# Moving one chunk's statistics of x1 from VectorE to ScalarE in the first stage of a mixing and scan kernel

## The chip, the cores and the metric

One core of a Trainium2 chip. The metric is the device time of one execution in microseconds; lower is better. The kernel before takes 773.96 us (median of 3 runs, 772.08 to 774.88).

## The reference

The input `x` has shape (16, 64, 128, 64): 16 samples, 64 rows h, 128 tokens n, 64 channels. Two layers follow each other, each with a group norm in front and a residual around it:

```
def _gn(v, G=32, eps=1e-05):
    g = v.reshape(B_, H_, W_, G, C_ // G)
    m = jnp.mean(g, axis=(1, 2, 4), keepdims=True)
    s = jnp.var(g, axis=(1, 2, 4), keepdims=True)
    return ((g - m) / jnp.sqrt(s + eps)).reshape(v.shape)

x = x + _L0_conv_ref(_gn(x), centers, spreads, bias)   # posmap (n x n, per head) mixes the tokens
x = x + _L1_conv_ref(_gn(x), conv_W)                   # scan over h: new = row + relu(conv1d(carry, W)), 9 taps
```

The second norm needs mean and variance of x1, the output of the first layer, per sample and pair of channels. These statistics of x1 are what the change is about.

## The kernel before, in words

The batch is worked on in two waves of W = 8 samples. The **first stage** mixes samples 0 to 7 alone, one after the other; the scan over 64 rows of wave 0 then runs while samples 8 to 15 are mixed in its gaps; last comes the scan of wave 1. Every engine has a program written out by hand, and its order is the order of the code; engines meet at semaphores. The change touches the first stage only.

A sample b is cut into CH = 4 chunks of 16 rows h. For each chunk, in this order:

- GpSimd scales the chunk of x by minus the reciprocal deviation of the first norm, in two halves (`scale_half`, L361, tile xs). The first half of a sample waits for `minus_rstd` (L681).
- TensorE mixes the tokens, 4 heads x 2 row halves in two passes (`mix_half`, L916), into `ps_mix` for chunks 0 and 2, into `ps_conv` for chunks 1 and 3.
- VectorE adds bias and residual (`mix_to_x1`, L699), which gives x1 in place.
- TensorE turns the chunk, 8 transposes (`turn_in`, L929, tile `ps_in`). It waits at L926 until ScalarE has emptied `ps_in` of the chunk before.
- ScalarE copies the turned chunk to `x1_paired` and adds the shift of the first norm, 4 activations on 64 partitions x 512 (`keep_in`, L469).
- VectorE takes the statistics of the kept chunk, 2 batch statistics on 128 x 512 (`stats2`, L706, tile st). After 8 of them `moments2` (L712) merges them into mean and variance.

Chunk 3 of a sample is turned and kept during the next sample's chunk 0; its statistics are taken at chunk 1 of the next sample.

Beside that run the statistics of x for a later sample: 16 batch statistics on 128 x 256 (`stats1`, L605), spread over the chunks of VectorE's program. Then comes a short chain for the first norm of sample b + 1: TensorE averages the means (`mean1_of`, after mixing chunk 1), VectorE takes deviations (L664), ScalarE squares them (L432), TensorE averages (`var1_of`, after mixing chunk 2), ScalarE takes the root (L438), VectorE its reciprocal (`guess1_of`, L670), ScalarE squares that (`square1_of`, L443), VectorE gives the ratio (L674) and `minus_rstd` (L681).

What is queued in which order is what matters here:

- ScalarE (L539): keep chunk 3 of b - 1; L432; keep chunk 0; L453; L438; L443; keep chunk 1; L448; keep chunk 2.
- TensorE (`alone_chunk`, L1009): chunk 0: mix 0, turn 3 of the sample before. Chunk 1: mix 1, mean1, turn 0. Chunk 2: mix 2, var1, turn 1, the group mean of b - 1. Chunk 3: mix 3, turn 2, `var2_of`, `shift1_of`. Then mix 0 of the next sample.
- VectorE (`alone_chunk`, L806): x1 of the chunk (L699), then a share of stats1, stats2 and the small steps.

Of the kernel before, what the change touches and what calls it, by code (L numbers as in the profile page):

```python
# [15 lines left out]
def mix_and_scan_kernel(nc: bass.Bass, x: bass.AP, centers: bass.AP, spreads: bass.AP,  # L16
# [5 lines left out]
    ACT = mybir.ActivationFunctionType  # L22
    AX = mybir.AxisListType

    B, H, N, C = x.shape
# [4 lines left out]
    P = 128  # L30
    J = N // 2
# [5 lines left out]
    W = B // 2  # L37
# [5 lines left out]
    CH = 4  # L43
    CR = H // CH
    CC = CR * C
    HR = CR // 2
    RG = 4
    GROUPS = STEPS // RG
    TU = 2 * CH
# [10 lines left out]
    with ExitStack() as ctx:  # L60
        def sb(name, shape, dt=f32):
            return ctx.enter_context(nc.sbuf_tensor(name, shape, dt))
# [4 lines left out]
        def sem(name):  # L67
            return ctx.enter_context(nc.semaphore(name))
# [14 lines left out]
        staged = sb("staged", [P, 2, NS * SW])  # L83
# [9 lines left out]
        minus_mean_rstd = sb("minus_mean_rstd", [P, 2, G, CG])  # L93
        shift1 = sb("shift1", [P, 2])
        st2 = sb("st2", [P, 2 * CH, 6])
        mv = sb("mv", [P, 2])
        dev_c = sb("dev_c", [P, 1])
        dev_c2 = sb("dev_c2", [P, 1])
# [83 lines left out]
        in_turned = sem("in_turned")  # L182
        in_kept = sem("in_kept")
        stats2_done = sem("stats2_done")
        mv_ready = sem("mv_ready")
        mean2_ps = sem("mean2_ps")
        dev_c_ready = sem("dev_c_ready")
# [16 lines left out]
        def x1_unit(wave, b, c, u):  # L204

            if wave == 1:
                v = x1_paired[:, bass.ds(b * (H * J) + (c * CR + u * HR) * J, HR * J)]
                return v.rearrange("p (h j) -> p h j", j=J)
            v = x1_paired[:, :].rearrange("p (h w j) -> p h w j", w=W, j=J)
            v = v[:, c * CR + u * HR:c * CR + (u + 1) * HR, bass.ds(b, 1), :]  # L210
            return v.rearrange("p h w j -> p h (w j)")

        def x1_chunk(wave, b, c):

            if wave == 1:
                v = x1_paired[:, bass.ds(b * (H * J) + c * CR * J, CR * J)]
                return v.rearrange("p (h j) -> p h j", j=J)
            v = x1_paired[:, :].rearrange("p (h w j) -> p h w j", w=W, j=J)
            return v[:, c * CR:(c + 1) * CR, b, :]
# [9 lines left out]
        def buf_of(b):  # L229

            return XB - 1 - b % XB
# [9 lines left out]
        def alone(eng, done):  # L241

            eng.wait_ge(done, 1)

        def held(eng, n):

            return n if isinstance(n, int) else eng.to_reg(n)

        def is_zero(n):
            return isinstance(n, int) and n == 0  # L250
# [173 lines left out]
        def _(act):  # L424
            for s in range(S):
                act.wait_ge(score_ready, s + 1)
                nc.scalar.activation(prob[:, s, :], score[:, s, :], ACT.Exp, bias=neg_max[:, s:s + 1],
                                     accum_out=exp_sum[:, s:s + 1]).then_inc(prob_ready, 1)
# [12 lines left out]
            def square1_of(b, halves=1):  # L441
                act.wait_ge(guess1_ready, b + 1)
                nc.scalar.activation(square1[:, :], guess1[:, :], ACT.Square,  # L443
                                     scale=math.sqrt(0.5 * halves / COUNT)).then_inc(square1_ready, 1)
# [8 lines left out]
                nc.scalar.activation(shift2[:, bass.ds(b, 1)], minus_mean2[:, :], ACT.Copy,  # L453
                                     scale=rstd2[:, bass.ds(b, 1)]).then_inc(shift2_ready, 1)

            def keep_in(b, k, wave, bw, c, first, count, free):

                if first == 0:
                    act.wait_ge(shift1_ready, b + 1)
                    chunks = held(act, b * CH + c + 1)  # L460
                    alone(act, setup_done)
                    if free is not None:
                        for s in range(NS):
                            act.wait_ge(total_ready[s], free)
                    act.wait_ge(in_turned, chunks)
                dst = x1_chunk(wave, bw, c)
                for r, q in ((0, 0), (0, 1), (1, 0), (1, 1))[first:first + count]:
                    src = ps_in[r * C:(r + 1) * C, :].rearrange("p (k j q) -> p q k j", k=HR, q=2)
                    ins = nc.scalar.activation(dst[q * C:(q + 1) * C, r:CR:2, :], src[:, q, :, :],  # L469
                                               ACT.Identity, bias=shift1[r * C:(r + 1) * C, k:k + 1])  # L470
                if first + count == 4:
                    ins.then_inc(in_kept, 1)

            def prep(b, e, i, prev, it):

# [63 lines left out]
            for b in range(W):  # L539
                if b > 0:  # L540
                    keep_in(b - 1, (b - 1) % 2, 0, b - 1, CH - 1, 0, 4, None)
                dev2_of(b + 1)
                keep_in(b, b % 2, 0, b, 0, 0, 4, None)
                if b > 1:
                    shift2_of(b - 2)
                std1_of(b + 1)
                square1_of(b + 1)
                keep_in(b, b % 2, 0, b, 1, 0, 4, None)
                if b > 0:
                    dev_c2_of(b - 1)  # L550
                keep_in(b, b % 2, 0, b, 2, 0, 4, None)
# [34 lines left out]
        def _(dve):  # L586
            nc.vector.memset(w_raw, 0.0).then_inc(w_zeroed, 1)
            nc.vector.memset(eps_col[:, :], EPS)
            nc.vector.memset(half_power[:, :], -0.5).then_inc(consts, 1)
            nc.vector.memset(ones_row, 1.0)  # L590
            nc.vector.memset(inv_p[:, :], 1.0 / P)
# [7 lines left out]
            def stats1(b, e, first, count):  # L599

                for c in range(CH):
                    dve.wait_ge(x_loaded[e][c], 16 * (b // XB + 1) if isinstance(b, int) and b <= W else 8 * b - 16 + 8 * e)
                v = x_bufs[e].rearrange("p (h m g e) -> p m h e g", m=G // 2, g=2, e=CG)
                for m in range(first, first + count):
                    ins = nc.vector.bn_stats(st1[:, 0, 2 * m:2 * m + 2, :].rearrange("p g k -> p (g k)"),  # L605
                                             v[:, m, :, :, :])
                if first + count == G // 2:
                    ins.then_inc(stats1_done, 1)
# [59 lines left out]
            def guess1_of(b):  # L668
                dve.wait_ge(std1_ready, b + 1)
                nc.vector.reciprocal(guess1[:, :], std1[:, :]).then_inc(guess1_ready, 1)  # L670
# [24 lines left out]
            def mix_to_x1(b, e, c, ps):  # L695
# [3 lines left out]
                nc.vector.scalar_tensor_tensor(v, ps[:, :].rearrange("p (s n) -> p n s", s=S),  # L699
                                               bias_col[:, 0:1], v, ALU.add, ALU.add).then_inc(x1_done, 1)  # L700

            def stats2(b, wave, bw, c, u):
                if c == 0 and u == 0 and not is_zero(b):
                    dve.wait_ge(mv_ready, b)
                dve.wait_ge(in_kept, b * CH + c + 1)
                nc.vector.bn_stats(st2[:, 2 * c + u, :], x1_unit(wave, bw, c, u)).then_inc(stats2_done, 1)  # L706

            def moments2(b):
                seen = held(dve, TU * b + TU)
                alone(dve, consts)  # L710
                dve.wait_ge(stats2_done, seen)
                nc.vector.bn_aggr(mv[:, :], st2[:, :, :].rearrange("p n k -> p (n k)")).then_inc(mv_ready, 1)  # L712

            def deviations2(b, wave):
                dve.wait_ge(mean2_ps, b + 1)
# [90 lines left out]
            def alone_chunk(b, c):  # L806

                e = buf_of(b)
                mix_to_x1(b, e, c, (ps_mix, ps_conv)[c % 2])
                nb, ne, nk = b + 1, buf_of(b + 1), (b + 1) % 2  # L810
                ahead = b + 2 <= W
                ae = buf_of(b + 2)
                if c == 0:
                    if b == 0:
                        stats1(nb, ne, 0, 9)
                    stats1(nb, ne, 9, 4)
                    if b > 0:
                        stats2(b - 1, 0, b - 1, 2, 0)
                        stats2(b - 1, 0, b - 1, 2, 1)
                    stats1(nb, ne, 13, 3)  # L820
                if c == 1:
                    dev_of(nb)
                    if b > 0:
                        stats2(b - 1, 0, b - 1, 3, 0)
                        stats2(b - 1, 0, b - 1, 3, 1)
                        moments2(b - 1)
                if c == 2:
                    stats2(b, 0, b, 0, 0)
                    guess1_of(nb)
                    if b > 0:  # L830
                        deviations2(b - 1, 0)
                    stats2(b, 0, b, 0, 1)
                    ratio1_of(nb)
                    if ahead:
                        stats1(b + 2, ae, 0, 1)
                    rstd1_of(nb, nk)
                    if ahead:
                        stats1(b + 2, ae, 1, 3)
                if c == 3:
                    mean_rstd1(nb, nk)  # L840
                    if ahead:
                        stats1(b + 2, ae, 4, 3)
                    stats2(b, 0, b, 1, 0)
                    if b > 0:
                        variance2(b - 1, 0)
                    stats2(b, 0, b, 1, 1)
                    keep_shift1(nb, nk)
                    if ahead:
                        stats1(b + 2, ae, 7, 2)

            dev_of(0, 2)
            guess1_of(0)
# [224 lines left out]
```

## Time and profile before

| | |
|---|---|
| median of 3 runs | 773.96 us |
| the profiled execution | 779.17 us, its span 777.4 us |
| busy over the span: TensorE, VectorE, ScalarE, GpSimd | 88%, 76%, 63%, 55% |
| first mixed chunk of sample 0 reaches VectorE | 29.5 us |
| first step of the scan on VectorE (L789) | 185.55 us |

The span is that of the profiled core, from the first instruction to the last; the execution's own time is 1.8 us longer, and it lies 5.2 us above the median. A group of instructions is given with its line, engine, operation, `output<-input`, shape and count. "Idle before" is the time its engine waited just ahead of it, with the instruction that released it. The granted clock is a share of full speed: 1.00 is 2.4 GHz, 0.50 is 1.2 GHz.

### The profile page before, as it was taken

To read this page: it belongs to the slowest core of one execution; us is meant where nothing else is said; L and a number is where in the kernel's file an instruction comes from. 1 tells how busy PE (TensorE), PEld (TensorE's weight loads), DVE (VectorE), ACT (ScalarE), POOL (GpSimd) and SP (SyncE) were. 2 spreads that over 40 slices of the span, in tenths; PEclk is the share of its full clock that TensorE was granted. 3 is DMA by queue.
4 is the path that set the end of the run, shared out by engine and by line. 5 is a ranking of instruction groups with operands and counts; after the bars stand their busy time and mean duration, and the time that the engine had idled before them with its cause. 6 is when DMAs were issued, how large, how long until landed. Compare 5 with 4: busy or idle time off the path is not lost.

```text
span 777.4 us, 18263 instructions
## 1 busy us (share of the span) xinstructions
PE 682.4 (88%) x5100; PEld 645.6 (83%) x5100; DVE 592.8 (76%) x1426; ACT 490.2 (63%) x854; POOL 431.0 (55%) x416
## 2 busy tenths in 40 slices
PE   1577777767999999999899999996999999999996
PEld 1466666657899898989799898995999999999995
DVE  7578999983878888797879888765666776776774
ACT  1165777776676777676676777746666666666661
POOL 1555556642666666665566666661555555555554
PEclk9888999997999999999999999998999999999999
DMA  9844656231455554554555543331444444444444
GB/s 185 155 109 109 134 113 134 55 82 30 80 104 102 107 105 77 106 98 85 98 100 101 106 79 50 52 53 28 70 75 73 72 69 76 72 68 75 72 72 78
DMA packets 412050, 68.18 MB, mean 88 GB/s; under 512 B 411988, under 2 KB 411988, under 8 KB 411988
## 3 DMA queue, kind: packets, MB, share of 16 engines
q1 hardware_dynamic: 359764, 61.17, 42.5%
q10 hardware_dynamic: 52224, 6.30, 5.2%
q8 instruction: 24, 0.39, 0.2%
q14 instruction: 38, 0.31, 0.2%
HBM read 33.85 MB, written 33.55 MB: 87 GB/s over the span
## 4 chain that ended last, share of the span: by engine, by line
PE 46%; DVE 23%; issue 13%; ACTq 6%; ACT 6%; SPq 3%; POOL 1%; DVEq 1%; DMA 0%; POOLq 0%
PE ps_conv L992 22%; PE ps_conv L996 11%; DVE st L605 7%; PE ps_mix L916 7%; ACTq L503 6%; PE ps_in L929 5%; DVE carry L789 3%; DVE st L706 3%; SPq L299 3%; DVE carry_l L799 2%; ACT carry_h L513 2%; DVE staged L776 2%; PE ps_small L906 2%; ACT x_paired L469 2%; DVE x_sb L699 2%
## 5 line engine op out<-in xcount | busy, mean ns | idle before, releaser
L388 POOL TENSOR_TENSOR total<-x_paired,carry 128x256 f32<-128x256 f32 x256 | 252.2, 985 | 237.8 <-DVE staged L776 230.6
L513 ACT ACTIVATE carry_h<-carry 128x256 fp32r<-128x256 f32 x252 | 105.3, 418 | 188.1 <-DVE carry L789 136.7
L491 ACT ACTIVATE rows<-x_paired,shift,rstd 128x256 f32 (+1 forms) x256 | 213.6, 843 | 0.2
L992 PE MATMUL ps_conv<-carry_h,wh 128*128 128x256 f32 x1280 | 204.7, 291 | 6.7 <-ACT carry_h L513 6.3
L996 PE MATMUL ps_conv<-carry_l,wh 128*128 128x256 f32 x1280 | 194.2, 282 | 0.3 <-DVE carry_l L799 0.3
L469 ACT ACTIVATE x_paired<-ps_in,shift 64x512 f32<-64x512 f32 (+1 forms) x256 | 174.8, 683 | 31.2 <-PE ps_in L929 26.6
L992 PE MATMUL ps_conv<-carry_h,wl 128*128 128x256 f32 x1280 | 194.2, 282 | 0.0
L992 PEld LDWEIGHTS ps_conv<-carry_h,wh 128*128 128x128 f32 x1280 | 171.4, 191 | 11.4 <-ACT carry_h L513 9.4
L799 DVE TENSOR_TENSOR carry_l<-carry,carry_h 128x256 fp32r<-128x256 f32 x252 | 134.6, 534 | 58.9 <-ACT carry_h L513 41.9
L992 PEld LDWEIGHTS ps_conv<-carry_h,wl 128*128 128x128 f32 x1280 | 171.4, 190 | 0.0
L996 PEld LDWEIGHTS ps_conv<-carry_l,wh 128*128 128x128 f32 x1280 | 170.7, 189 | 0.6 <-DVE carry_l L799 0.6
L361 POOL TENSOR_TENSOR xs<-x_sb,minus_rstd 128x512 f32<-128x512 f32 x104 | 139.8, 1356 | 45.7 <-DVE minus_rstd L681 34.1
L789 DVE SCALAR_TENSOR_TENSOR carry<-ps_conv,rows 128x256 f32<-128x256 f32 x256 | 106.7, 417 | 74.2 <-PE ps_conv L996 62.8
L776 DVE STREAM_TRANSPOSE staged<-total 128x256 f32<-128x256 f32 x256 | 110.7, 433 | 5.4 <-DMA out_dram<-staged 5.0
L916 PE MATMUL ps_mix<-xs,mix 128*128 128x256 f32 x384 | 105.3, 407 | 0.6 <-DVE x_sb L699 0.4
L706 DVE BATCH_NORM_STATS2 st<-x_paired 128x6 f32<-128x512 f32 (+1 forms) x128 | 85.7, 683 | 8.2 <-ACT x_paired L469 8.2
L916 PEld LDWEIGHTS ps_mix<-xs,mix 128*128 128x128 f32 x384 | 71.6, 202 | 9.7 <-POOL xs L361 1.8
L605 DVE BATCH_NORM_STATS2 st<-x_sb 128x6 f32<-128x256 f32 x208 | 73.8, 405 | 0.0
L929 PE MATMUL ps_in<-ident,x_sb 128*128 128x128 f32 x416 | 55.9, 278 | 15.7 <-ACT x_paired L469 11.4
L929 PEld LDWEIGHTS ps_in<-ident,x_sb 128*128 128x128 f32 x416 | 48.6, 145 | 22.2 <-issue 17.9
L699 DVE SCALAR_TENSOR_TENSOR x_sb<-ps_mix,bias_col,x_sb 128x1024 f32<-128x1024 f32 x42 | 53.6, 1276 | 5.9 <-PE ps_mix L916 5.8
L361 POOL TENSOR_TENSOR xs<-rows,minus_rstd 128x512 f32<-128x512 f32 x24 | 31.2, 1335 | 33.1 <-DVE minus_rstd L681 31.7
(89 smaller groups left out, 290.2 us busy)
## 6 DMA issues: line engine op xcount, KB each, us to landing
x_sb<-in_x_dram SPq DMA_DIRECT2D x52, 512.0 KB, 4.1
out_dram<-staged SPq DMA_DIRECT2D x832, 32.0 KB, 1.6
rows<-in_x_dram SPq DMA_DIRECT2D x12, 512.0 KB, 4.0
out_dram<-staged ACTq DMA_DIRECT2D x192, 32.0 KB, 1.8
x_paired<-in_L_conv_W_dram SPq DMA_DIRECT2D x2, 80.0 KB, 2.9
x_paired<-in_L_conv_W_dram SPq DMA_DIRECT2D x2, 64.0 KB, 2.6
x_paired<-v_attention_centers_dram SPq DMA_DIRECT2D x1, 0.0 KB
x_paired<-v_attention_spreads_dram SPq DMA_DIRECT2D x1, 0.0 KB
```

The source lines that it names most:

```text
L361: nc.gpsimd.tensor_tensor(xs[:, c % 2, heads, :, :].rearrange("p s h v -> p h v s"), src, minus_rstd1[:, k, m:G:2].unsqueeze(1).unsqueeze( ...
L388: nc.gpsimd.tensor_tensor(total[s][:, :].rearrange("p (w j) -> p w j", w=WS), x1_rows(wave, it, i, 1, s * WS, WS)[:, 0, :, :], carry[s][:, ...
L469: ins = nc.scalar.activation(dst[q * C:(q + 1) * C, r:CR:2, :], src[:, q, :, :], ACT.Identity, bias=shift1[r * C:(r + 1) * C, k:k + 1])
L491: nc.scalar.activation(rows[:, g % 2, :, w // WS, :, w % WS], x1_rows(wave, it, g * RG, RG, w, 1)[:, :, 0, :], ACT.Identity, scale=rstd2[: ...
L605: ins = nc.vector.bn_stats(st1[:, 0, 2 * m:2 * m + 2, :].rearrange("p g k -> p (g k)"), v[:, m, :, :, :])
L776: nc.vector.transpose(staged[:, buf, s * SW:(s + 1) * SW], total[s][:, :]).then_inc(out_flipped[s], 1)
L789: nc.vector.scalar_tensor_tensor(carry[s][:, :], ps_conv[:, s * BANK:s * BANK + SW], 0.0, rows[:, (i // RG) % 2, i % RG, s, :, :].rearrang ...
L799: nc.vector.tensor_tensor(carry_l[s][:, EDGE:EDGE + J, :].rearrange("p j w -> p (j w)"), carry[s][:, :], carry_h[s][:, EDGE:EDGE + J, :].r ...
L916: ins = nc.tensor.matmul(ps[:, s * CR * V:(s + 1) * CR * V], mix[:, s, :], xs[:, c % 2, s, :, :].rearrange("p h v -> p (h v)"), start=True ...
L929: ins = nc.tensor.transpose(ps_in[:, k * P:(k + 1) * P], x_bufs[e][:, at:at + P], ident[:, :])
L992: nc.tensor.matmul(ps_conv[:, s * BANK:s * BANK + SW], w[:, d, :], carry_h[s][:, d:d + J, :].rearrange("p j w -> p (j w)"), start=(w is wh ...
L996: ins = nc.tensor.matmul(ps_conv[:, s * BANK:s * BANK + SW], wh[:, d, :], carry_l[s][:, d:d + J, :].rearrange("p j w -> p (j w)"), start=F ...
```

## The change

In the first stage the statistics of chunk 0 of each sample move to ScalarE. The 4 activations that keep chunk 0 also give their sums (`accum_out`, each to a column of `sums2`). A new step, `squares2`, stands in ScalarE's program behind `square1_of` and ahead of the copy of chunk 1: it scales the two sums to means, written into the statistics tile st2 (slot 0 or 7 by turns); it waits for that; then two activations on 128 x 512 square the kept chunk about its mean and give the sums of squares, also into st2. The squared values go to `staged`, which is not used in this stage. VectorE no longer takes chunk 0's two batch statistics, and merges 7 slots in place of 8: six of its own and one from ScalarE. VectorE's stats1 are placed anew: three more of them stand in chunk 2, and one fewer before the copy of the shift in chunk 3. The second wave is as it was.

```diff
-            def keep_in(b, k, wave, bw, c, first, count, free):
+            def keep_in(b, k, wave, bw, c, first, count, free, sums=None):
...
                     ins = nc.scalar.activation(dst[q * C:(q + 1) * C, r:CR:2, :], src[:, q, :, :],
-                                               ACT.Identity, bias=shift1[r * C:(r + 1) * C, k:k + 1])
+                                               ACT.Identity, bias=shift1[r * C:(r + 1) * C, k:k + 1],
+                                               accum_out=None if sums is None else sums[q * C:(q + 1) * C, r:r + 1])
                 if first + count == 4:
                     ins.then_inc(in_kept, 1)
+
+            def squares2(b):
+
+                slot = (TU - 1) * (b % 2)
+                act.wait_ge(in_kept, b * CH + 1)
+                if b > 1:
+                    act.wait_ge(mv_ready, b - 1)
+                nc.scalar.activation(st2[:, slot, 1:6:3], sums2[:, :], ACT.Copy,
+                                     scale=1.0 / (HR * J)).then_inc(mean_c_ready, 1)
+                act.wait_ge(mean_c_ready, b + 1)
+                for r in range(2):
+                    nc.scalar.activation(staged[:, r, :], x1_chunk(0, b, 0)[:, r:CR:2, :],
+                                         ACT.Square, scale=-1.0, bias=st2[:, slot, 1 + 3 * r:2 + 3 * r],
+                                         accum_out=st2[:, slot, 2 + 3 * r:3 + 3 * r]).then_inc(squares2_done, 1)
...
-                keep_in(b, b % 2, 0, b, 0, 0, 4, None)
+                if b > 0:
+                    act.wait_ge(squares2_done, 2 * b)
+                keep_in(b, b % 2, 0, b, 0, 0, 4, None, sums2)
                 if b > 1:
                     shift2_of(b - 2)
                 std1_of(b + 1)
                 square1_of(b + 1)
+                squares2(b)
                 keep_in(b, b % 2, 0, b, 1, 0, 4, None)
...
             def moments2(b):
-                seen = held(dve, TU * b + TU)
+                first, last = 0, TU
+                seen = held(dve, TU * b + TU - 2 * W)
+                if wave_chunk(b):
+                    seen = (TU - 2) * (b + 1)
+                    first, last = b % 2, TU - 1 + b % 2
                 alone(dve, consts)
+                if wave_chunk(b):
+                    dve.wait_ge(squares2_done, 2 * (b + 1))
                 dve.wait_ge(stats2_done, seen)
-                nc.vector.bn_aggr(mv[:, :], st2[:, :, :].rearrange("p n k -> p (n k)")).then_inc(mv_ready, 1)
+                nc.vector.bn_aggr(mv[:, :], st2[:, first:last, :].rearrange("p n k -> p (n k)")).then_inc(mv_ready, 1)
...
                 if c == 2:
-                    stats2(b, 0, b, 0, 0)
                     guess1_of(nb)
+                    if ahead:
+                        stats1(b + 2, ae, 0, 3)
                     if b > 0:
                         deviations2(b - 1, 0)
-                    stats2(b, 0, b, 0, 1)
+                    if ahead:
+                        stats1(b + 2, ae, 3, 1)
                     ratio1_of(nb)
                     if ahead:
-                        stats1(b + 2, ae, 0, 1)
+                        stats1(b + 2, ae, 4, 1)
                     rstd1_of(nb, nk)
                     if ahead:
-                        stats1(b + 2, ae, 1, 3)
+                        stats1(b + 2, ae, 5, 1)
```

VectorE's order at chunk 2 of a sample, from x1 of chunk 2 to x1 of chunk 3, before:

```order
L699 SCALAR_TENSOR_TENSOR x_sb<-ps_mix,bias_col,x_sb 128x1024
L706 BN_STATS st<-x_paired 128x6
L670 RECIPROCAL guess<-std 128x32
L718 TENSOR_TENSOR dev_c<-mv,ps_out 128x1
L719 TENSOR_SCALAR minus_mean<-ps_out 128x1
L706 BN_STATS st<-x_paired 128x6
L674 SCALAR_TENSOR_TENSOR ps_small<-ps_small,square 128x32
L605 BN_STATS st<-rows 128x6
L681 SCALAR_TENSOR_TENSOR minus_rstd<-ps_small,guess 128x32
L605 BN_STATS st<-rows 128x6 x3
L699 SCALAR_TENSOR_TENSOR x_sb<-ps_conv,bias_col,x_sb 128x1024
```

The same place in the changed kernel (its line numbers are larger, L721 for L699, L692 for L670):

```order
L721 SCALAR_TENSOR_TENSOR x_sb<-ps_mix,bias_col,x_sb 128x1024
L692 RECIPROCAL guess<-std 128x32
L627 BN_STATS st<-rows 128x6 x3
L750 TENSOR_TENSOR dev_c<-mv,ps_out 128x1
L751 TENSOR_SCALAR minus_mean<-ps_out 128x1
L627 BN_STATS st<-rows 128x6
L696 SCALAR_TENSOR_TENSOR ps_small<-ps_small,square 128x32
L627 BN_STATS st<-rows 128x6
L703 SCALAR_TENSOR_TENSOR minus_rstd<-ps_small,guess 128x32
L627 BN_STATS st<-rows 128x6
L721 SCALAR_TENSOR_TENSOR x_sb<-ps_conv,bias_col,x_sb 128x1024
```

The two statistics of x1 are gone, one of them from in front of the reciprocal; six statistics of x stand here in place of four, four of them between the reciprocal and the ratio.

ScalarE's order from the copy of chunk 0 to the copies of chunks 2 and 3, before:

```order
L469 ACTIVATE x_paired<-ps_in,shift 64x8x64 x4
L453 ACTIVATE shift<-minus_mean,rstd 128x1
L438 ACTIVATE std<-ps_small,eps_col 128x32
L443 ACTIVATE square<-guess 128x32
L469 ACTIVATE x_paired<-ps_in,shift 64x8x64 x4
L448 ACTIVATE dev_c<-dev_c 128x1
L469 ACTIVATE x_paired<-ps_in,shift 64x8x64 x8
```

And in the changed kernel:

```order
L472 ACTIVATE x_paired,sums<-ps_in,shift 64x8x64 x4
L456 ACTIVATE shift<-minus_mean,rstd 128x1
L441 ACTIVATE std<-ps_small,eps_col 128x32
L446 ACTIVATE square<-guess 128x32
L484 ACTIVATE st<-sums 128x2
L488 ACTIVATE staged,st<-x_paired,st 128x512 x2
L472 ACTIVATE x_paired<-ps_in,shift 64x8x64 x4
L451 ACTIVATE dev_c<-dev_c 128x1
L472 ACTIVATE x_paired<-ps_in,shift 64x8x64 x8
```

Three activations, and a wait for the first of them, now stand between the square of the guess and the copy of chunk 1.

## Rows read from the trace of the kernel before

**Rows 1.** One sample of the first stage: busy us per engine (count); clock share, DMA.
```profile
104.94:121.97 17.03, 12.65 (x78) 10.78 (x78) 16.36 (x39) 12.16 (x22) 10.69 (x10) 1.00 0.57 124
```

**Rows 2.** The chain of waits in the same stretch, shares by line.
```profile
by line: DVE st L605 28.6%; issue 20.1%; DVE x_sb L699 15.2%; DVE st L706 12.5%; PE ps_in L929 9.3%; PE ps_mix L916 8.3%; PE ps_small L906 1.8%; DVEq L602 1.3%; DVE minus_mean_rstd L686 0.9%; DVE ps_small L674 0.9%; DVE minus_rstd L681 0.8%
```

**Rows 3.** Timeline, samples 4 to 5: start us, duration us, engine, line, operation, [idle before <-releaser].
```profile
111.26 2.77 ACT L469 ACTIVATE x_paired<-ps_in,shift 64x512 f32<-64x512 f32 x4
...
112.89 1.28 DVE L699 SCALAR_TENSOR_TENSOR x_sb<-ps_mix,bias_col,x_sb 128x1024 f32<-128x1024 f32 x1 [0.25 <-PE ps_mix L916]
...
114.13 0.69 DVE L706 BATCH_NORM_STATS2 st<-x_paired 128x6 f32<-128x512 f32 x1
...
114.74 0.34 DVE L670 RECIPROCAL guess<-std 128x32 f32<-128x32 f32 x1
...
115.11 0.23 ACT L443 ACTIVATE square<-guess 128x32 f32<-128x32 f32 x1 [0.45 <-DVE guess L670]
...
115.36 2.77 ACT L469 ACTIVATE x_paired<-ps_in,shift 64x512 f32<-64x512 f32 x4
...
116.81 5.08 POOL L361 TENSOR_TENSOR xs<-x_sb,minus_rstd 128x512 f32<-128x512 f32 x4 [6.04 <-DVE minus_rstd L681]
...
118.27 1.06 PE L929 MATMUL ps_in<-ident,x_sb 128*128 128x128 f32 x8 [1.08 <-ACT x_paired L469]
...
119.45 2.77 ACT L469 ACTIVATE x_paired<-ps_in,shift 64x512 f32<-64x512 f32 x4 [1.10 <-PE ps_in L929]
...
119.76 1.97 PE L916 MATMUL ps_mix<-xs,mix 128*128 128x256 f32 x8
...
121.97 1.27 DVE L699 SCALAR_TENSOR_TENSOR x_sb<-ps_mix,bias_col,x_sb 128x1024 f32<-128x1024 f32 x1
...
123.55 2.76 ACT L469 ACTIVATE x_paired<-ps_in,shift 64x512 f32<-64x512 f32 x4 [1.33 <-PE ps_in L929]
...
126.87 0.38 PE L906 MATMUL ps_small<-st,inv_p 128*128 128x32 f32 x2 [1.71 <-DVE st L605]
...
128.30 2.77 ACT L469 ACTIVATE x_paired<-ps_in,shift 64x512 f32<-64x512 f32 x4
```

**Rows 4.** Groups by line over the whole span: count | busy, mean ns | idle before.
```profile
L513 ACT ACTIVATE carry_h<-carry 128x256 fp32r<-128x256 f32 x252 | 105.3, 418 | 188.1 <-DVE carry L789 136.7
L491 ACT ACTIVATE rows<-x_paired,shift,rstd 128x256 f32 (+1 forms) x256 | 213.6, 843 | 0.2
...
L706 DVE BATCH_NORM_STATS2 st<-x_paired 128x6 f32<-128x512 f32 (+1 forms) x128 | 85.7, 683 | 8.2 <-ACT x_paired L469 8.2
```

**Rows 5.** Timeline of ScalarE in the setup, activations that also sum.
```profile
8.39 0.39 ACT L427 ACTIVATE x_paired<-x_paired 128x128 f32<-128x128 f32 x1
8.68 0.19 ACT L427 ACTIVATION_READ_ACCUMULATOR x_paired<-x_paired 128x1 f32 x1
8.78 0.39 ACT L427 ACTIVATE x_paired<-x_paired 128x128 f32<-128x128 f32 x1
```

**Rows 6.** Timeline of samples 0 and 1, around chunk 1's copy.
```profile
43.08 0.34 DVE L670 RECIPROCAL guess<-std 128x32 f32<-128x32 f32 x1
...
43.45 0.23 ACT L443 ACTIVATE square<-guess 128x32 f32<-128x32 f32 x1 [1.52 <-DVE guess L670]
...
46.48 1.25 PE L929 MATMUL ps_in<-ident,rows 128*128 128x128 f32 x8 [2.13 <-ACT x_paired L469]
...
51.22 1.28 DVE L699 SCALAR_TENSOR_TENSOR x_sb<-ps_mix,bias_col,x_sb 128x1024 f32<-128x1024 f32 x1 [1.48 <-PE ps_mix L916]
```

**Rows 7.** Timeline one sample on.
```profile
65.88 1.06 PE L929 MATMUL ps_in<-ident,x_sb 128*128 128x128 f32 x8 [1.84 <-ACT x_paired L469]
...
70.86 1.28 DVE L699 SCALAR_TENSOR_TENSOR x_sb<-ps_mix,bias_col,x_sb 128x1024 f32<-128x1024 f32 x1 [1.53 <-PE ps_mix L916]
```

**Rows 8.** TensorE's busy time and granted clock in one stretch of 2 us.
```profile
68.00:70.00 2.00, 2.00 (x6) 0.50 1.07 243
```

**Rows 9.** Timeline of TensorE behind the last sample of the stage.
```profile
173.50 1.93 PE L929 MATMUL ps_in<-ident,x_sb 128*128 128x128 f32 x8 [2.47 <-ACT x_paired L469]
```

More of the change, by code:

```diff
@@ L95, in mix_and_scan_kernel @@
         st2 = sb("st2", [P, 2 * CH, 6])
+        sums2 = sb("sums2", [P, 2])
         mv = sb("mv", [P, 2])
@@ L184, in mix_and_scan_kernel @@
         stats2_done = sem("stats2_done")
+        mean_c_ready = sem("mean_c_ready")
+        squares2_done = sem("squares2_done")
         mv_ready = sem("mv_ready")
@@ L588, in _ @@
             nc.vector.memset(eps_col[:, :], EPS)
+            nc.vector.memset(st2[:, 0:TU:TU - 1, 0:6:3], HR * J)
             nc.vector.memset(half_power[:, :], -0.5).then_inc(consts, 1)
@@ L700, in mix_to_x1, with wave_chunk @@
                                                bias_col[:, 0:1], v, ALU.add, ALU.add).then_inc(x1_done, 1)
+            def wave_chunk(b):
+                return 1 if isinstance(b, int) and b < W else 0
             def stats2(b, wave, bw, c, u):
-                if c == 0 and u == 0 and not is_zero(b):
+                if c == wave_chunk(b) and u == 0 and not is_zero(b):
                     dve.wait_ge(mv_ready, b)
                 dve.wait_ge(in_kept, b * CH + c + 1)
-                nc.vector.bn_stats(st2[:, 2 * c + u, :], x1_unit(wave, bw, c, u)).then_inc(stats2_done, 1)
+                nc.vector.bn_stats(st2[:, 2 * c + u - wave_chunk(b), :], x1_unit(wave, bw, c, u)).then_inc(stats2_done, 1)
             def moments2(b):
-                seen = held(dve, TU * b + TU)
+                first, last = 0, TU
[3 more added lines that the diff above has]
+                    first, last = b % 2, TU - 1 + b % 2
                 alone(dve, consts)
+                if wave_chunk(b):
+                    dve.wait_ge(squares2_done, 2 * (b + 1))
                 dve.wait_ge(stats2_done, seen)
-                nc.vector.bn_aggr(mv[:, :], st2[:, :, :].rearrange("p n k -> p (n k)")).then_inc(mv_ready, 1)
+                nc.vector.bn_aggr(mv[:, :], st2[:, first:last, :].rearrange("p n k -> p (n k)")).then_inc(mv_ready, 1)
             def deviations2(b, wave):
@@ L841, in alone_chunk @@
                     if ahead:
-                        stats1(b + 2, ae, 4, 3)
+                        stats1(b + 2, ae, 6, 3)
                     stats2(b, 0, b, 1, 0)
@@ L847, in alone_chunk @@
                     keep_shift1(nb, nk)
-                    if ahead:
-                        stats1(b + 2, ae, 7, 2)
             dev_of(0, 2)
```

## The prediction

> **What bounds the kernel now.** I read three views, all in the first stage, because the change touches nothing behind it. The table of stretches says how full each engine is over one sample: the sample takes 17.03 us, VectorE is busy 16.36 of them (96%), ScalarE 12.16, TensorE 12.65, GpSimd 10.69, the clock is full [rows 1]. The chain of waits gives the same picture: VectorE's statistics and x1 steps hold most of it, and ScalarE does not appear [rows 2]. So far VectorE looks like the bound, and taking two statistics from it like a gain.
>
> The third view is the timeline of one sample [rows 3], read for what waits behind ScalarE. Its four copies stand 4.1 us apart (111.26, 115.36, 119.45, 123.55) and the last gap is 4.75 us (to 128.30). In every 4.1 us, 2.77 are the copy itself and the rest is the turning of the next chunk, which may not begin before the copy ends: 115.36 + 2.77 = 118.13, and TensorE starts turning at 118.27 after 1.08 us idle, released by ScalarE. This ring of ScalarE and TensorE needs 4 x 4.1 = 16.4 us per sample, 96% of the period too. And TensorE's queue holds more behind that turning: the small products, then the mix of the next sample's chunk 0 at 119.76, ready at 121.73. VectorE takes it at 121.97, so the mix was 0.24 us early, and with a pick-up of some 0.05 us the slack is **0.2 us**. From there VectorE needs until about 126.7 for the last statistic of x, TensorE follows at 126.87 (released by it), turns chunk 0, and ScalarE starts on it at 128.30. That closes a second ring: copy 0, square of the guess, copy 1, turning of chunk 2, mix of chunk 0, x1, statistics of x, turning of chunk 0. It passes through both engines, and only 0.2 us of it is slack.
>
> **What the change removes.** Two batch statistics at L706 per sample, 683 ns each in the row [rows 4], about 0.60 us each from start to start (the reciprocal follows the statistic of 114.13 at 114.74 [rows 3]): 1.2 us per sample. Where they stood, between x1 of chunk 2 and the ratio, VectorE lies in the second ring only by the reciprocal. The reciprocal of 114.74 waits for ScalarE's root, which starts behind the copy and ends about 114.67, so taking the statistic from in front of it returns 0.1 us at most; I take nothing. In samples 0 and 1 the reciprocal was late through VectorE itself: ScalarE's square had been idle 1.52 us ahead of it [rows 6]. There the removed statistic gives back 0.6 us, once in each.
>
> **What it adds, all on ScalarE.**
> - Sums of the four copies. In the setup an activation that sums is followed by a read of the accumulator: 8.39, 8.68, then 8.78 [rows 5]. The read adds 0.10 us from start to start; its own duration is 0.19, which is the upper end. 4 x 0.10 = 0.40.
> - The scaling to means and the wait for it. The nearest small activation takes 0.23 us (at 115.11 [rows 3]). I take 0.23.
> - Two squares of 128 x 512. L513 takes 418 ns for 256 columns, L491 843 ns for 256 columns written with a stride [rows 4], and the copy L469 2.77 / 4 = 0.69 for 512. Source and target of the squares lie in runs of 64 and more, as the copy's do, so I take 0.61 from start to start plus 0.10 for the read: 1.42 for both. Upper end, at L491's rate: 2 x (1.69 + 0.19) = 3.8.
>
> The sum is 0.40 + 0.23 + 1.42 = **2.05 us** per sample, all of it ahead of copy 1, so on both rings. Per sample:
> - Samples 2 to 6: 2.05 less the slack of 0.2 is 1.85, times five 9.25.
> - Samples 0 and 1: the sums (0.40) lie in ScalarE's wait for the guess, and 0.6 comes back: 2.05 - 0.40 - 0.60 = 1.05 each, 2.1.
> - Sample 7: behind it ScalarE keeps copying and normalising up to the scan's first step, so 2.05 in full.
>
> That makes 13.4 us. Moved work costs nothing: the six statistics of x that now stand at chunk 2 delay `minus_rstd` and with it GpSimd's first half by some 0.9 us against copy 0. GpSimd's halves start at 116.81 and take 5.08 / 4 = 1.27 each, so chunk 0 is scaled at 119.4 while TensorE reaches it at 119.76; TensorE now comes 2.05 later and GpSimd about 1.3 (0.4 of the sums and 0.9), so it stays early. If not, this would cost up to its 0.9 us per sample. The one memset added in the setup and the merge over 7 slots I take as nothing. There is no new DMA.
>
> **TensorE's clock.** TensorE's idle time ahead of the turning of chunk 2 was 1.08 us [rows 3]. It grows by 2.05 less the 0.40 by which mixing chunk 3 also moves: **2.7 us**. What such a pause did in this trace: after 2.13 us [rows 6] and 1.84 us [rows 7] at this very place, and after 2.47 us behind the last sample [rows 9] (1.93 us there for 8 transposes that take 1.06), TensorE ran at the lower level, 0.50 or 1.2 GHz [rows 8]; after 1.71 us (ahead of 126.87 [rows 3]) it did not. The price stands in the time from turning to x1: 51.22 - 46.48 = 4.74 and 70.86 - 65.88 = 4.98 against 121.97 - 118.27 - 0.2 = 3.5, so 1.24 and 1.48 us, mean 1.36. In samples 0 and 1 it is paid already; six pauses are new. I expect the lower level in part of them, as the fall does not always meet the mix of chunk 0, and take 3.3 of six: 4.5 us. None would be 0, all six 8.2.
>
> **Sum.** 13.4 + 4.5 = 17.9 us. The profiled execution would go from 779.17 to 797.1, and the median, 5.2 us below it, from 773.96 to **791.9**.
>
> **Rivals.**
> - *The clock holds.* The period of one sample grows to 18.9 us but the mix stays at 2.4 GHz: 774.0 + 13.4 = 787.4. For it: the full-clock periods with a pause of 1.71 us each. Against: three of the four long pauses above. With an insertion at 1.9 us it would be 786.
> - *VectorE is the bound, and its relief counts.* 8 x 1.2 = 9.6 us less: 764.4. For it: 96% busy and the chain of waits [rows 1, 2]. The Trainium skill (Perfetto Trace Analysis, Identifying the Most-Contended Engine, and Optimizing Scalar/DVE Operations) says the engine with the highest occupancy is the one to work on first, and that handing work to ScalarE may pay once VectorE is saturated; this case's busy shares fit that rule. Against: ScalarE's insertion would have to cost less than the 0.2 us of slack, or stand off both rings; it stands ahead of copy 1, and copy 1 releases TensorE. The point from which this decides is ScalarE's time between the square and copy 1: under 0.2 us VectorE's gain shows, above it ScalarE's loss.
> - *Loss and gain cancel*, because part of ScalarE's 4.87 us idle per sample (17.03 - 12.16) takes up the insertion: about 772. Against: that idle time is waiting for the turning, which itself waits for the copy.
> - *The squares are slow*, at L491's rate: 3.8 in place of 1.42, so 8 x 2.4 = 19 us more: 807 to 811. Against: the copy at L469 writes the same tile at 0.69.
> - *The change doesn't do what it says*: excluded, the order shows two statistics per sample gone and three activations added.
>
> **Chances.** Path longer and clock lower in part: 0.62. Clock holds: 0.22. Slow squares: 0.07. Cancel: 0.05. Relief counts: 0.04. A measurement of this kernel can tell about 0.5% (3.9 us) from no change. Faster by over that: 0.04; within: 0.05; slower: 0.91. The range takes in the two likeliest cases with their bounds: low 13.4 with an insertion of 1.9 (less 1.2) and no lower clock, 786, less 2 for the spread of the runs; high 13.4 + 8.2 and reads at 0.14 in place of 0.10 (6 x 0.04 x 8 = 2), 798, plus 2. So 784 to 800.
>
> **What would show it.** The distance of x1 of chunk 0 from sample to sample: 18.9 at full clock, 20.3 with the lower one, in place of 17.03. VectorE's busy share of a sample under 85%, with idle time ahead of the reciprocal (about 1 us) and ahead of x1 of chunk 0 (over 1 us), which had none. TensorE idle 2.7 us ahead of turning chunk 2. The group of squares at 0.70 us each. The scan's first step near 203 in place of 185.55, and nothing changed behind it. Wrong I would be if copy 1 began as early as before, that is if the squares had found idle time, or if the period stayed at 17 us.

## The result, and the profile after

The changed kernel takes 801.97 us (median of 4 runs, 799.3 to 802.71) against 774.42 us of the kernel before on the same chip: 1.0351 times as long, 95% interval 1.0312 to 1.0389, so 27.55 us slower. The sign was as forecast. The forecast was 791.9 us with a range of 784 to 800, so the loss was 1.5 times the 17.9 us forecast and the time lies above the range.

The profiled execution took 802.71 us, its span 800.9 us. The scan's first step on VectorE begins at 211.87 us; it was at 185.55. So the first stage lost 26.3 us, and behind it the two profiles differ by 2.8 us the other way (591.8 and 589.0 us). The loss by samples, from x1 of chunk 0 to that of the next sample:

| sample | before, us | after, us | difference |
|---|---|---|---|
| 0 | 21.72 | 22.93 | 1.21 |
| 1 | 19.64 | 22.56 | 2.92 |
| 2 | 17.05 | 20.64 | 3.59 |
| 3, 4 | 17.03 | 20.63 | 3.60 each |
| 5 | 17.04 | 21.42 | 4.38 |
| 6 | 17.03 | 21.94 | 4.91 |
| 7 and on to the scan | 29.51 | 31.62 | 2.11 |

The table of stretches of the changed kernel, for samples 3, 5 and 6 (us, then busy time and count of TensorE, its weight loads, VectorE, ScalarE, GpSimd; granted clock; share and GB/s of DMA), answers to [rows 1]:

```profile
95.63:116.26 20.63, 14.14 (x80) 12.09 (x79) 15.38 (x36) 14.26 (x30) 10.71 (x9) 0.92 0.48 103
...
136.89:158.31 21.42, 16.32 (x80) 13.79 (x79) 15.25 (x37) 14.26 (x30) 10.71 (x9) 0.81 0.47 99
158.31:180.25 21.94, 16.51 (x80) 14.28 (x79) 15.39 (x36) 14.26 (x30) 10.75 (x9) 0.81 0.11 24
```

VectorE's busy time fell from 16.36 to 15.38 us, ScalarE's rose from 12.16 to 14.26, as intended. But the sample takes 20.63 us, and neither engine is near that. The granted clock, 1.00 before, is 0.92 and 0.81.

The chain of waits over sample 3 answers to [rows 2]. ScalarE did not appear in it; its copies now hold the largest share:

```profile
by line: ACT x_paired L472 24.7%; PE ps_mix L948 18.9%; issue 17.9%; DVE st L627 11.5%; PE ps_in L961 9.6%; ACT staged L488 4.5%; DVE st L732 3.5%; PE ps_small L938 3.2%; DVE guess L692 1.8%; PE ps_out L938 1.6%; ACT shift L456 1.4%; ACT st
```

The timeline of that sample answers to [rows 3 to 5] (start us, duration us, engine, line, operation, idle time before and its releaser):

```profile
101.97 0.68 ACT L472 ACTIVATE x_paired<-ps_in,shift 64x512 f32<-64x512 f32 x1
102.55 0.19 ACT L472 ACTIVATION_READ_ACCUMULATOR x_paired<-ps_in,shift 64x1 f32 x1
102.76 0.68 ACT L472 ACTIVATE x_paired<-ps_in,shift 64x512 f32<-64x512 f32 x1
...
103.45 0.20 ACT L472 ACTIVATION_READ_ACCUMULATOR x_paired<-ps_in,shift 64x1 f32 x1
...
103.66 0.69 ACT L472 ACTIVATE x_paired<-ps_in,shift 64x512 f32<-64x512 f32 x1
...
105.37 0.30 ACT L456 ACTIVATE shift<-minus_mean,rstd 128x1 f32<-128x1 f32 x1
...
106.01 0.35 DVE L692 RECIPROCAL guess<-std 128x32 f32<-128x32 f32 x1 [1.14 <-ACT std L441]
...
106.40 0.23 ACT L446 ACTIVATE square<-guess 128x32 f32<-128x32 f32 x1 [0.42 <-DVE guess L692]
...
106.54 0.19 ACT L484 ACTIVATE st<-sums 128x2 f32<-128x2 f32 x1
...
106.76 0.72 ACT L488 ACTIVATE staged<-x_paired,st 128x512 f32<-128x512 f32 x1
...
107.48 0.71 ACT L488 ACTIVATE staged<-x_paired,st 128x512 f32<-128x512 f32 x1
...
108.18 2.75 ACT L472 ACTIVATE x_paired<-ps_in,shift 64x512 f32<-64x512 f32 x4
...
108.35 5.08 POOL L364 TENSOR_TENSOR xs<-x_sb,minus_rstd 128x512 f32<-128x512 f32 x4 [7.52 <-DVE minus_rstd L703]
...
111.08 1.06 PE L961 MATMUL ps_in<-ident,rows 128*128 128x128 f32 x8 [2.57 <-ACT x_paired L472]
...
112.26 2.77 ACT L472 ACTIVATE x_paired<-ps_in,shift 64x512 f32<-64x512 f32 x4 [1.10 <-PE ps_in L961]
...
112.62 3.61 PE L948 MATMUL ps_mix<-xs,mix 128*128 128x256 f32 x8
...
116.26 1.28 DVE L721 SCALAR_TENSOR_TENSOR x_sb<-ps_mix,bias_col,x_sb 128x1024 f32<-128x1024 f32 x1 [2.92 <-PE ps_mix L948]
```

Read it down ScalarE. From the first activation of copy 0 to L456 it was 2.80 us before; now it is 105.37 - 101.97 = 3.40. From the square of the guess to copy 1 it was 0.25; now it is 108.18 - 106.40 = 1.78. These two, 0.60 and 1.53, are the insertion: **2.13 us**. VectorE waits 1.14 us for the root, and later for the mix. TensorE is idle 2.57 us ahead of turning chunk 2 (111.08), still turns at full speed, and then mixes chunk 0 in 3.61 us where it took 1.97. From turning to x1 that makes 116.26 - 111.08 = 5.18 us, where it was 3.70.

Two groups of the profile's page: copies as before at 683 ns, and 16 batch statistics fewer, at the duration they had [rows 4].

```profile
L472 ACT ACTIVATE x_paired<-ps_in,shift 64x512 f32<-64x512 f32 (+1 forms) x256 | 174.9, 683 | 41.0 <-PE ps_in L961 36.8
...
L732 DVE BATCH_NORM_STATS2 st<-x_paired 128x6 f32<-128x512 f32 (+1 forms) x112 | 75.0, 684 | 9.5 <-ACT x_paired L472 9.2
```

### The profile page after: what moved, and what is told of

Its sections match the earlier page's. It is cut to its first block, busy times and chain, and to the rows that moved or that the text cites. A ratio compares the mean times of both kernels' runs of the same rounds, so it can differ in the third digit from the quotient of the medians.

```text
span 800.9 us, 18347 instructions
## 1 busy us (share of the span) xinstructions
PE 696.3 (87%) x5100; PEld 659.0 (82%) x5100; DVE 585.6 (73%) x1411; ACT 507.0 (63%) x926; POOL 431.3 (54%) x416
## 4 chain that ended last, share of the span: by engine, by line
PE 46%; DVE 18%; issue 14%; ACT 11%; ACTq 6%; SPq 3%; POOL 1%; DVEq 1%; DMA 0%; POOLq 0%
PE ps_conv L1024 21%; PE ps_conv L1028 10%; PE ps_mix L948 8%; ACTq L521 6%; DVE st L627 6%; ACT x_paired L472 5%; PE ps_in L961 5%; DVE carry L821 3%; SPq L302 3%; ACT carry_h L531 2%; PE ps_small L938 2%; DVE carry_l L831 2%; DVE st L732 2%; DVE staged L808 2%; ACT rows L509 2%
## 5 line engine op out<-in xcount | busy, mean ns | idle before, releaser
L948 PE MATMUL ps_mix<-xs,mix 128*128 128x256 f32 x384 | 114.0, 434 | 0.2 <-POOL xs L364 0.2
L948 PEld LDWEIGHTS ps_mix<-xs,mix 128*128 128x128 f32 x384 | 77.8, 219 | 11.4 <-POOL xs L364 1.4
L732 DVE BATCH_NORM_STATS2 st<-x_paired 128x6 f32<-128x512 f32 (+1 forms) x112 | 75.0, 684 | 9.5 <-ACT x_paired L472 9.2
L961 PE MATMUL ps_in<-ident,x_sb 128*128 128x128 f32 x416 | 58.0, 285 | 21.9 <-ACT x_paired L472 20.5
L961 PEld LDWEIGHTS ps_in<-ident,x_sb 128*128 128x128 f32 x416 | 50.6, 149 | 28.0 <-issue 18.4
L721 DVE SCALAR_TENSOR_TENSOR x_sb<-ps_mix,bias_col,x_sb 128x1024 f32<-128x1024 f32 x42 | 53.6, 1277 | 19.1 <-PE ps_mix L948 19.0
```

What stands on the lines that cost most here:

```text
L948: ins = nc.tensor.matmul(ps[:, s * CR * V:(s + 1) * CR * V], mix[:, s, :], xs[:, c % 2, s, :, :].rearrange("p h v -> p (h v)"), start=True ...
L961: ins = nc.tensor.transpose(ps_in[:, k * P:(k + 1) * P], x_bufs[e][:, at:at + P], ident[:, :])
```

## The experiments

Each time is a median of the kernel's runs, and each ratio is to the kernel before, measured beside it: 776.25 us for the first four kernels, 774.93 us for the last four. Times of samples are those of the one profiled execution.

### Filling TensorE's pause

On the changed kernel:

```diff
+                if c == 3:
+                    pe.wait_ge(x1_done, b * CH + 3)
+                    for s in range(S):
+                        nc.tensor.matmul(ps_mix[:, 0:256], mix[:, s, :],
+                                         mix[:, 0:2, :].rearrange("p s m -> p (s m)"), start=True, stop=True)
                 if c > 0:
                     turn_in(b, buf_of(b), c - 1)
```

> The changed kernel with four products of 256 columns (0.49 us each, 1.97 us) that nobody reads, on TensorE ahead of turning chunk 2 in the first stage. They fill the pause of 2.57 us. Theory (the path is longer by 2.11 us, and the pause takes TensorE to 1.2 GHz just where the mix of chunk 0 is on the path): the granted clock stays at 1.00, samples 2 to 6 stand 18.9 us apart in place of 20.6 to 21.9, and the time is 774.4 + 13.8 = 788, or 1 to 3 less if samples 0 and 1 keep the clock too. Rival (the clock is not what costs 12 us; some wait on ScalarE or GpSimd is longer than I read): it stays at 800 to 804, for the fillers only use idle time.

Measured: 788.92 us, 1.0173 times before (1.0133 to 1.0213), as expected. More work on TensorE took 13 us off the changed kernel. Its timeline in sample 3, then the table of stretches for the next sample:

```profile
101.04 1.89 PE L1056 MATMUL ps_mix<-mix 128*128 128x256 f32 x8
...
103.78 1.07 PE L961 MATMUL ps_in<-ident,rows 128*128 128x128 f32 x8 [0.84 <-ACT x_paired L472]
...
105.27 1.97 PE L948 MATMUL ps_mix<-xs,mix 128*128 128x256 f32 x8
...
107.28 1.28 DVE L721 SCALAR_TENSOR_TENSOR x_sb<-ps_mix,bias_col,x_sb 128x1024 f32<-128x1024 f32 x1 [1.24 <-PE ps_mix L948]
```

```profile
107.28:126.22 18.94, 14.38 (x86) 12.31 (x86) 15.38 (x36) 14.24 (x31) 10.72 (x9) 1.00 0.50 112
```

The unread products (101.04) leave 0.84 us of pause, the mix of chunk 0 takes 1.97 us again, and the granted clock is 1.00. Samples 2 to 6 take 18.94 us each. So two losses are told apart: 18.94 - 17.03 = 1.91 us per sample is the longer path at full clock, and the rest of the 3.6 to 4.9 us hung on the clock. Samples 0 and 1 became 1.67 and 3.94 us shorter than in the changed kernel (21.26 and 18.62 us), so there too the clock had cost time.

### The same work on ScalarE, in its waits

On the changed kernel, `squares2` split in two by `r`, with the scaling in the first part:

```diff
                 square1_of(b + 1)
-                squares2(b)
                 keep_in(b, b % 2, 0, b, 1, 0, 4, None)
                 if b > 0:
                     dev_c2_of(b - 1)
+                squares2(b, 0)
                 keep_in(b, b % 2, 0, b, 2, 0, 4, None)
+                squares2(b, 1)
```

> The changed kernel with the same work on ScalarE in another place: the scaling to means and the first square after copy 1 and L451, the second square after copy 2, where ScalarE waits 1.1 to 1.3 us for the next turning. Theory (place on the ring decides): only the four reads of the accumulator, 0.60 us, stay ahead of copy 1. Less the slack of 0.2 that is 0.4 in five samples, nothing or a gain of 0.5 in samples 0 and 1, some 1.3 in sample 7, and TensorE's pause stays near 1.1 us, so the clock holds: 775 to 779. Rival (ScalarE's added load costs wherever it stands): 800 to 802. Rival (VectorE's relief then shows): 766 to 770.

Measured: 777.68 us, 1.0023 times before (1.0004 to 1.0042). The sum of ScalarE's work is the same as in the changed kernel, and 24 us of the loss are gone. The timeline of sample 3 shows why:

```profile
95.03 0.23 ACT L446 ACTIVATE square<-guess 128x32 f32<-128x32 f32 x1 [0.42 <-DVE guess L694]
...
95.30 2.77 ACT L472 ACTIVATE x_paired<-ps_in,shift 64x512 f32<-64x512 f32 x4
...
98.20 0.19 ACT L485 ACTIVATE st<-sums 128x2 f32<-128x2 f32 x1
98.21 1.06 PE L963 MATMUL ps_in<-ident,rows 128*128 128x128 f32 x8 [1.08 <-ACT x_paired L472]
...
98.42 0.72 ACT L489 ACTIVATE staged<-x_paired,st 128x512 f32<-128x512 f32 x1
...
99.39 2.77 ACT L472 ACTIVATE x_paired<-ps_in,shift 64x512 f32<-64x512 f32 x4 [0.16 <-PE ps_in L963]
...
101.71 1.28 DVE L723 SCALAR_TENSOR_TENSOR x_sb<-ps_mix,bias_col,x_sb 128x1024 f32<-128x1024 f32 x1 [0.77 <-PE ps_mix L950]
...
102.19 0.72 ACT L489 ACTIVATE staged<-x_paired,st 128x512 f32<-128x512 f32 x1
```

The square of the guess (95.03) is followed by copy 1 after 0.27 us, and TensorE's pause ahead of turning chunk 2 is 1.08 us, as before the change. Scaling and first square stand at 98.20 and 98.42. The copy of chunk 2 (99.39) still starts 1.18 us behind the turning, having waited 0.16 us for it; in the kernel before it had waited 1.10. Four of samples 2 to 6 take 17.45 us, 0.42 more than before. Against VectorE's relief alone (16.85, the next experiment) they take 0.60 more: the four accumulator reads in full, and nothing for scaling and squares. So work of ScalarE is free where its engine waits for the turning, and costs in full where the turning waits for it.

Two things lie behind the near zero of the total. Samples 0 and 1 were 1.9 and 2.2 us shorter than before (19.82 and 17.46 us), which hides a part of what the reads cost. And one sample, 4, took 18.28 us: TensorE's mix of chunk 1 took 3.55 us in it (at 112.61) in place of 1.97, behind a pause of only 1.57 us.

### VectorE's relief alone

On the changed kernel, without sums, scaling and squares, so that chunk 0 of samples 0 to 7 is left out of the second norm's statistics:

```diff
-                squares2(b)
...
-                    act.wait_ge(squares2_done, 2 * b)
-                keep_in(b, b % 2, 0, b, 0, 0, 4, None, sums2)
+                keep_in(b, b % 2, 0, b, 0, 0, 4, None)
...
-                    first, last = b % 2, TU - 1 + b % 2
+                    first, last = 1, TU - 1
...
-                    dve.wait_ge(squares2_done, 2 * (b + 1))
```

> The changed kernel without anything new on ScalarE: chunk 0 of samples 0 to 7 is left out of the second norm's statistics, and VectorE has the changed order. Theory (two rings, VectorE's relief is worth only the slack of ScalarE's ring): 0.2 us in five samples and 0.6 in samples 0 and 1, 772, at most 770. Rival (VectorE is the bound): 8 x 1.2 = 9.6 less, 765.

Measured: 771.41 us, 0.995 times before (0.993 to 0.997), 4.8 us less. The scan's first step:

```profile
179.85 0.42 DVE L816 SCALAR_TENSOR_TENSOR carry<-ps_conv,rows 128x256 f32<-128x256 f32 x1 [1.93 <-ACT rows L509]
```

It comes 5.70 us earlier than the 185.55 before, so the gain lies in the first stage. The period of a sample:

```profile
99.80:116.65 16.85, 12.65 (x78) 10.78 (x78) 15.16 (x37) 12.17 (x22) 10.71 (x10) 1.00 0.56 125
```

VectorE's busy time is down by 1.20 us per sample, the period by 0.18 (16.85 against 17.03), the slack of 0.2 us. That rules out the rival by which the relief counts in full. Most of the gain stands in samples 0 and 1, which became 1.58 and 2.80 us shorter (20.14 and 16.84 us) where 0.6 us each was expected:

```profile
46.21 1.06 PE L956 MATMUL ps_in<-ident,rows 128*128 128x128 f32 x8 [1.32 <-ACT x_paired L472]
...
47.25 1.97 PE L943 MATMUL ps_mix<-xs,mix 128*128 128x256 f32 x8
```

In sample 0 TensorE's pause ahead of turning chunk 2 was 1.32 us in place of 2.13 [rows 6], the mix behind it took 1.97 us in place of 3.36, and from there to the end of sample 6 the clock stayed at 1.00. What the first two samples gained beyond the 0.6 us goes with TensorE's clock. The 4.8 us are a little over the 4.4 that the expectation gave as the most (770, from 774.42).

### ScalarE's load alone

On the kernel before, the same additions to `keep_in` and the same `squares2` at the same place, with a tile of its own, `stx`, in place of st2:

```diff
+        stx = sb("stx", [P, 2, 6])
...
                 square1_of(b + 1)
+                squares2(b)
                 keep_in(b, b % 2, 0, b, 1, 0, 4, None)
```

> The kernel before with ScalarE's added work alone: sums with the copies of chunk 0, scaling, two squares, all into a tile that nobody reads; VectorE as before with all eight statistics in their old order. Theory (the loss is the insertion ahead of copy 1): as the changed kernel, 800 to 804, in samples 0 and 1 up to 0.6 us each longer. Rival (VectorE's new order, with three statistics of x between the reciprocal and the ratio, costs by making minus_rstd late): near 790 or less, since the order is the old one.

Measured: 802.79 us, 1.0343 times before (1.0288 to 1.0398). This is the changed kernel's whole loss (1.0351) with VectorE's old order and all its eight statistics, so beside this load VectorE's relief gave nothing that shows. The rival by which VectorE's new order costs (it makes `minus_rstd` later) falls. The timeline:

```profile
95.08 1.28 DVE L719 SCALAR_TENSOR_TENSOR rows<-ps_mix,bias_col,rows 128x1024 f32<-128x1024 f32 x1 [2.14 <-PE ps_mix L936]
...
110.55 1.06 PE L949 MATMUL ps_in<-ident,rows 128*128 128x128 f32 x8 [2.60 <-ACT x_paired L473]
...
115.67 1.28 DVE L719 SCALAR_TENSOR_TENSOR x_sb<-ps_mix,bias_col,x_sb 128x1024 f32<-128x1024 f32 x1 [2.20 <-PE ps_mix L936]
```

The same 20.6 us between samples (95.08 to 115.67), the same pause ahead of turning chunk 2, 2.60 us.

### Taking the other ring's load away

On the kernel before, only VectorE's order:

```diff
-                    stats1(nb, ne, 9, 4)
-                    if b > 0:
-                        stats2(b - 1, 0, b - 1, 2, 0)
-                        stats2(b - 1, 0, b - 1, 2, 1)
-                    stats1(nb, ne, 13, 3)
+                    stats1(nb, ne, 9, 7)
                 if c == 1:
                     dev_of(nb)
                     if b > 0:
+                        stats2(b - 1, 0, b - 1, 2, 0)
+                        stats2(b - 1, 0, b - 1, 2, 1)
                         stats2(b - 1, 0, b - 1, 3, 0)
...
                 if c == 2:
-                    stats2(b, 0, b, 0, 0)
                     guess1_of(nb)
+                    stats2(b, 0, b, 0, 0)
```

> The kernel before with nothing on ScalarE and VectorE's order changed: the two statistics of chunk 2 of the sample before go from the middle of chunk 0 (where TensorE's first mean waits for the last statistic of x) into chunk 1, and the reciprocal goes ahead of the statistic of chunk 0. Theory (two rings): the ring through VectorE loses 1.18 us, so ScalarE's ring of 16.4 us and VectorE's own 16.4 set the pace: 16.4 to 16.6 in place of 17.03 in five samples, 0.5 or more in samples 0 and 1, so 3 to 4 us less than before. Rival (VectorE's total work is the bound, order doesn't matter): no change within 0.3 us per sample.

Measured: 768.8 us, 0.992 times before (0.990 to 0.994). It beats both kernels: 6.1 us less than before, some 33 less than the change. (No run joins this order with the late squares of the second experiment.) The period of a sample:

```profile
99.98:116.39 16.41, 12.81 (x78) 10.86 (x78) 16.12 (x40) 12.20 (x22) 10.71 (x10) 1.00 0.62 129
```

16.4 us is what the four copies at 4.1 us set [rows 3]; samples 1 to 6 stand 16.2 to 16.5 us apart. No engine got less to do. The gain was larger than the 3 to 4 us expected, since sample 1 fell from 19.64 to 16.18 us, 3.46 of the 7.6 us by which the scan starts earlier: TensorE kept 2.4 GHz from 53 us on, where before it had been at 1.2 GHz again around 68 us [rows 8].

> The same with two products of 256 columns that nobody reads (0.98 us) on TensorE ahead of turning chunk 2. Theory (a pause of 1.8 to 2.1 us there cost 1.2 to 1.5 us of clock in samples 0 and 1 of the kernel before): another 1 to 3 us less than the reordered kernel alone. Rival (the clock in the first samples hangs on something else, or the fillers delay the turning): no gain, or 0.1 us lost per sample.

Two unread products ahead of turning chunk 2 (the edit of the first experiment with `range(2)`) on top of that: 768.25 us, 0.9914 times before (0.9895 to 0.9934). Sample 0 became 1.1 us shorter (20.28 against 21.38), with the mix of chunk 0 in 1.97 us in place of 3.25; the total is not told from the reordered kernel's. The expected 1 to 3 us came out at 0.9, just under, and by the scan's first step alone (177.00 against 177.94).

### How long a pause TensorE bears

The edit of the first experiment with `range(1)` and `range(2)` on the changed kernel.

> The changed kernel with one unread product in the pause ahead of turning chunk 2, which leaves 2.1 us of it. Theory (the length of the pause decides whether TensorE falls to 1.2 GHz): pauses of 2.13, 1.84 and 2.47 us were followed by the lower level and one of 2.14 was not, so a part of the samples is still slow: 791 to 801. If any work in the pause is enough: 788.

Measured: 798.51 us, 1.0285 times before (1.0249 to 1.0321), as expected. Behind the same pause of 2.15 us the mix of chunk 0 took 1.97 us in one sample (at 132.49) and 3.76 us in another (at 111.74).

> The same with two unread products, which leave 1.6 us of the pause. In the kernel before, pauses of 1.71 us kept the full clock. Theory: the clock holds from sample 2 on and the time is 787 to 790, as with four. Rival (the share of work, not the pause, decides, and two products are too few): 792 or more.

Measured: 795.73 us, 1.0252 times before (1.0203 to 1.0301), its runs from 788.6 to 798.5, with pauses of 1.71 us in samples 2 to 6. This expectation failed. The timeline of two samples of the second kernel that follow each other, first one where the clock held, then one where it fell:

```profile
104.10 1.06 PE L961 MATMUL ps_in<-ident,rows 128*128 128x128 f32 x8 [1.57 <-ACT x_paired L472]
...
109.68 1.06 PE L961 MATMUL ps_in<-ident,rows 128*128 128x128 f32 x8 [1.71 <-ACT x_paired L472]
...
111.17 1.97 PE L948 MATMUL ps_mix<-xs,mix 128*128 128x256 f32 x8
```

```profile
123.04 1.06 PE L961 MATMUL ps_in<-ident,x_sb 128*128 128x128 f32 x8 [1.57 <-ACT x_paired L472]
...
128.63 1.06 PE L961 MATMUL ps_in<-ident,x_sb 128*128 128x128 f32 x8 [1.71 <-ACT x_paired L472]
...
130.12 3.42 PE L948 MATMUL ps_mix<-xs,mix 128*128 128x256 f32 x8
```

Ahead of both stands the same 1.71 us of idle time, and the mix of chunk 0 takes 1.97 us in the one and 3.42 us in the other. So the length of the pause alone does not decide. TensorE's work in the sample ahead looks alike in both too: the turning of chunk 1 stands 5.6 us before each, with the same 1.57 us of idle time, and the turning of chunk 2 one sample earlier 18.95 us before each. The time came out where the rival had it, but its reason, the share of work, is not shown by two samples that are alike. What decides stays open.

## Why the prediction was wrong, by its steps

**The bound.** Two rings with 0.2 us of slack between them: right. VectorE's relief alone brought 0.18 us per sample in samples 2 to 6, the path at full clock grew by 1.91 us (1.85 forecast), and with VectorE's ring relieved the period went to the 16.4 us of the copies. VectorE's 96% busy, and the chain of waits that named it, hid a ring of ScalarE and TensorE that was as tight. The Trainium skill (Perfetto Trace Analysis, Identifying the Most-Contended Engine) says to work first on the engine with the highest occupancy. This case does not bear that out: the rival that the prediction built for it gave 764; the relief alone measured 771, the change 802.

**The insertion.** 2.05 us forecast, 2.13 measured: right as a sum, by two errors of opposite sign. The sums of the four copies cost 0.60 in place of 0.40, the scaling and squares 1.53 in place of 1.65 (with the squares at 0.71 each from start to start, as forecast). Sample 7 lost 2.11 (2.05 forecast), sample 0 1.21 (1.05 forecast).

**The moved work.** Right to cost nothing. GpSimd's first half starts at 108.35, and with 1.27 us to a half chunk 0 is scaled by 110.9, well before TensorE mixes it at 112.62. ScalarE's load alone gave the same time without that move.

**TensorE's clock: the term that failed.** It was "3.3 of six: 4.5 us" at 1.36 us each. Taking the path at its 1.91 us, samples 2 to 4 lost 1.7 us each to the clock, sample 5 2.5 and sample 6 3.0, and sample 1, where I took the price as paid already, another 1.9 beyond the 1.05 forecast. That is 12.4 us. Two things were off. The clock fell, and cost time, behind the pause ahead of turning chunk 2 in each of samples 2 to 6, not in half of them; in sample 7 it cost nothing, its 2.11 us being the path alone. And its price was read from samples 0 and 1 of the kernel before, where the time from turning to x1 was 4.74 and 4.98 us; here it was 5.18 in samples 2 to 4, and in samples 5 and 6 the lower level also reached a second mix or the turning itself. The pause was well forecast (2.7 us, measured 2.57), and filling it gave back 13 us, so the mechanism was right and only its size was off. Why the clock falls behind one pause and not behind a like one stays open. The range was built with "all six: 8.2 us" as its upper bound, which was no bound: the price per pause was itself unknown, and samples 0 and 1 could pay more.

**From the stage to the median.** The first stage lost 26.3 us where 17.9 were forecast, 8.4 more: 7.9 by the clock (12.4 against 4.5), 0.5 by the path. Behind the stage 2.8 us came back; none were forecast, and no run explains them. And the profiled execution of the changed kernel lies 0.7 us above its median, where the prediction carried over the 5.2 us of the kernel before, which makes 4.5. Together 8.4 - 2.8 + 4.5 = 10.1 us, the distance from 791.9 to 801.97. Without the last term the time would have come out at 797.5, inside the range, and by luck, for the clock's term would be as far off as it is.

**The rivals.** "The clock holds" at 787.4 is what the filled kernel shows (788.9). The relief counting in full, loss and gain cancelling and slow squares all fell.

## What to carry to other kernels

An engine at 96% with idle time spread thin says nothing about how tight the next ring is: follow each wait once around until it meets itself, add up the times, and price an insertion on the ring that it stands on. Against VectorE's relief alone (771.4 us), ScalarE's added work cost 31 us where all of it stood ahead of the copy that TensorE waits for (802.0), and 6 us with scaling and squares in ScalarE's own waits (777.7). Reordering VectorE's small steps, with nothing offloaded, gained 6. When a change lengthens TensorE's repeated pauses, price the lower clock for every one of them, over all of TensorE's work on the path behind, and for samples that already fall.

## What the runs showed of the hardware that was not expected

In these runs the read of the accumulator comes later when the activation writes to other partitions than it reads. In the timeline above, the copy of 101.97 goes from partitions 0 to 63 to the same ones, and its read starts 0.58 us after it; the copy of 102.76 goes from partitions 0 to 63 to 64 to 127, and its read starts 0.69 us after it. From one copy to the next that is 0.79 and 0.90 us, against 0.69 without sums. The copies of 103.66 and 104.57 repeat the pair the other way round. The sums in the setup, from which the price of 0.10 us was read [rows 5], stay in their partitions.

And a filler of work that nobody reads can make a kernel faster: four products of 256 columns in each of 8 samples took 13 us off the changed kernel.
